# When GpSimd issues the next chunk loads, and where three other transfers stand, in a Perceiver block

## The reference

```python
x = x + softmax(layernorm(x) @ ctx.T) @ ctx              # ctx: 25088 x 2048
h = layernorm(x)
q, k, v = h @ Wq + bq, h @ Wk + bk, h @ Wv + bv          # 32 heads of 64 for q, 8 for k and v
s = softmax(einsum('bsdh,bseh->bsde', q, repeat(k, 4)) / 8)   # 64 x 64 for each token, over the heads
x = x + einsum('bsde,bseh->bsdh', s, repeat(v, 4))
h = layernorm(x)
route = top-2 of softmax(h @ W_gate.T), 8 experts, normalised
x = x + h @ W_base.T + b_base + sum_e route_e * (h @ A_e.T) @ B_e.T   # rank 16
```

## Time and profile before

| | us |
|---|---|
| three runs | 2582.25, 2589.11, 2597.52 (median 2589.11) |
| profiled execution | 2590.12, span 2588.5 |
| busy in the span | PE 2487.6, PEld 2031.1, DVE 1953.2, POOL 1422.9, ACT 1091.7 |
| mean granted clock of TensorE | 0.979 |

### The profile page before, as it was taken

How to read it: one execution, slowest core, us unless ns; L and a number is a source line. 1 busy time by engine, 2 the same in 40 slices (tenths; PEclk the granted TensorE clock), 3 DMA queues, 4 the chain that set the end, 5 groups by cost and what they waited for, 6 DMA issues and landing times.

```text
span 2588.5 us, 36100 instructions
## 1 busy us (share of the span) xinstructions
PE 2487.6 (96%) x11446; PEld 2031.1 (78%) x11446; DVE 1953.2 (75%) x2693; ACT 1091.7 (42%) x1576; POOL 1422.9 (55%) x1060
## 2 busy tenths in 40 slices
PE   6999999999999999999999999999999999997796
PEld 4788888888887888888888888888888888775574
DVE  7888787888877788788888787887878787642335
ACT  4444444444443444444444444444444444333331
POOL 4466666666665556565556655565655555512323
PEclk9999999999999999999999999999999999999877
DMA  9888888787888887898888888888888886685312
GB/s 236 220 219 205 229 205 229 207 228 207 228 216 218 205 216 204 215 220 218 212 223 206 211 209 220 217 205 214 223 216 214 215 220 201 148 155 130 111 61 73
DMA packets 421111, 518.22 MB, mean 200 GB/s; under 512 B 54406, under 2 KB 296070, under 8 KB 418440
## 3 DMA queue, kind: packets, MB, share of 16 engines
q1 hardware_dynamic: 411080, 475.66, 74.7%
q0 software_dynamic: 9984, 41.95, 4.6%
HBM read 488.71 MB, written 28.84 MB: 200 GB/s over the span
## 4 chain that ended last, share of the span: by engine, by line
PE 89%; DMA 4%; DVE 3%; POOL 2%; ACT 1%; issue 1%; SPq 1%; DVEq 0%; ACTq 0%; POOLq 0%
PE ps L1381 29%; PE ps L1383 29%; PE ps L1382 29%; DMA tr<-wt_dram 2%; PE ps L1390 2%; POOL ch_lo L646 1%; DMA raw<-in_ctx_dram 1%; ACT ch_hi L837 1%; DMA tr<-wp_dram 1%; SPq L405 1%; DVE ch_lo L1028 1%; POOL tr L641 0%; POOL x_b L697 0%; DVE tr L1024 0%; DVE acc L1147 0%
## 5 line engine op out<-in xcount | busy, mean ns | idle before, releaser
L578 POOL TENSOR_TENSOR nat_lo<-raw,nat_hi 128x512 fp32r<-128x512 f32 x784 | 1162.5, 1512 | 894.3 <-ACT nat_hi L735 863.3
L1028 DVE TENSOR_TENSOR ch_lo<-tr,ch_hi 128x512 fp32r<-128x512 f32 x784 | 837.8, 1069 | 341.9 <-ACT ch_hi L724 341.8
L724 ACT CAST ch_hi<-tr 128x512 fp32r<-128x512 f32 x784 | 476.3, 621 | 796.7 <-PE ps L1383 788.1
L1381 PE MATMUL ps<-ch_hi,xt_hi 128*128 128x512 f32 x1696 | 681.6, 402 | 24.1 <-DVE ch_lo L1192 9.4
L1382 PE MATMUL ps<-ch_lo,xt_hi 128*128 128x512 f32 x1696 | 665.6, 392 | 0.0
L1383 PE MATMUL ps<-ch_hi,xt_lo 128*128 128x512 f32 x1696 | 665.5, 392 | 0.0
L1381 PE MATMUL ps<-nat_hi,pt_hi 128*128 128x512 f32 x1568 | 614.4, 392 | 8.2 <-DVE pt_lo L977 7.3
L1383 PE MATMUL ps<-nat_hi,pt_lo 128*128 128x512 f32 x1568 | 611.2, 390 | 0.0
L1382 PE MATMUL ps<-nat_lo,pt_hi 128*128 128x512 f32 x1568 | 610.7, 389 | 0.0
L1024 DVE STREAM_TRANSPOSE tr<-quart 128x512 f32<-128x512 f32 x784 | 546.9, 698 | 0.0
L735 ACT CAST nat_hi<-raw 128x2048 fp32r<-128x2048 f32 x196 | 374.5, 1911 | 208.1 <-PE ps L1383 195.1
(11 more groups left out here) (181 smaller groups left out, 1462.5 us busy)
## 6 DMA issues: line engine op xcount, KB each, us to landing
quart<-in_ctx_dram SPq DMA_DIRECT2D x392, 512.0 KB, 8.2
raw<-in_ctx_dram SPq DMA_DIRECT2D x196, 1024.0 KB, 9.0
wq_in<-in_L_attn_Wq_dram POOLq DMA_DIRECT2D x16, 1024.0 KB, 6.4
win<-in_L_ffn_W_base_dram SPq DMA_DIRECT2D x64, 256.0 KB, 6.9
wt_dram<-stage SPq DMA_DIRECT2D x64, 256.0 KB, 7.6
tr<-wt_dram POOLq DMA_DIRECT2D x64, 256.0 KB, 4.2
wq_dram<-wq_out POOLq DMA_DIRECT2D x16, 256.0 KB, 2.3
wp_dram<-stage SPq DMA_DIRECT2D x16, 256.0 KB, 10.1
```

The costliest lines, as they stand in the source:

```text
L578: last = pool.tensor_tensor(nat_lo[:, j, t], raw[:, j % 2, t], nat_hi[:, j, t].bitcast(F32), ALU.subtract)
L724: act.copy(ch_hi[:, c % RING_CH, :], tr[:, c % RING_TR, :]).then_inc(chunk_hi, 1)
L1028: dve.tensor_tensor(ch_lo[:, c % RING_CH, :], tr[:, c % RING_TR, :], ch_hi[:, c % RING_CH, :].bitcast(F32), ALU.subtract).then_inc(chunk_s ...
L1381: pe.matmul(out_, a_hi, b_hi, start=start, stop=False)
```

## The change

POOL's low part of chunk w stands behind the loads of w + 1, w + 2 and w + 3. LoRA's B has its own buffer (8 KB a partition) and is loaded in two halves, at the end of the last two turns; b_base is loaded right behind the q loads. The four turned pieces of W_base use two buffers in turn, and each of the five stores has its own semaphore. The routed sums are transposed after chunks 6 and 7 instead of 11 and 12, v after 9 and 11 instead of 7 and 9. x2 plus b_base is made in eight pieces of 512 columns. The space for the descriptors of GpSimd's transfers is set to 4096 bytes a partition.

```diff
+        stages = (stage, sb("stage_b", [P, 4 * P]))
+        b_nat = sb("b_nat", [P, DC, ER])
...
-        b_nat = put(at_lo + 20 * KIB, "b_nat", [P, DC, ER])
...
-        wt_stored = sem("wt_stored")
+        wt_stored = [sem(f"wt_stored{k}") for k in range(5)]
...
                 if step == 1:
-                    sp.wait_ge(wt_stored, m * 80 + 80)
+                    for k in (3, 4):
+                        sp.wait_ge(wt_stored[k], m * 16 + 16)
                     load_win(m + 1)
...
+            def load_expert(e):
+                sp.dma_start(b_nat[:, :, e * RANK:(e + 1) * RANK],
+                             lora_b[e].rearrange("(o p) r -> p o r", p=P)).then_inc(b_loaded, 16)
+
             next_block(REST[0], LAST_M)
+            for e in range(EXPERTS // 2):
+                load_expert(e)
...
             sp.dma_start(x_nat[:], x_dram).then_inc(x_again, 16)
+            for e in range(EXPERTS // 2, EXPERTS):
+                load_expert(e)
             sp.wait_ge(chunk_transposed, DC * NB)
...
             sp.wait_ge(qkv_done, 3 * TT)
-            for e in range(EXPERTS):
-                sp.dma_start(b_nat[:, :, e * RANK:(e + 1) * RANK],
-                             lora_b[e].rearrange("(o p) r -> p o r", p=P)).then_inc(b_loaded, 16)
-            sp.wait_ge(plain_done, H_B + DC // 4)
             sp.dma_start(b_base_all[:], b_base.unsqueeze(0).broadcast_to([P, OUTF])).then_inc(bias_loaded, 16)
...
-                pool.wait_ge(wt_stored, m * 80 + 64)
+                pool.wait_ge(wt_stored[2], m * 16 + 16)
...
-            lo_base(3)
             pool.wait_ge(qkv_done, 3 * TT)
...
-            for w in range(RING_TR, BASE_W):
-                load_base(w)
-                if by_pool(w):
-                    lo_base(w)
-            for w in range(BASE_W, ALL_W):
-                load_base(w)
-                if by_pool(w):
-                    lo_base(w)
-                if w - BASE_W in X2B_AFTER:
-                    t, half = X2B_AFTER[w - BASE_W]
-                    cols = slice(half * OUTF // 2, (half + 1) * OUTF // 2)
+            for w in range(RING_TR, ALL_W + 3):
+                if w < ALL_W:
+                    load_base(w)
+                if by_pool(w - 3):
+                    lo_base(w - 3)
+                for piece in X2B_AFTER.get(w - 3 - BASE_W, ()):
+                    t, ob = piece // FB, piece % FB
+                    cols = slice(ob * KB, (ob + 1) * KB)
...
                 elif k < 4:
-                    dve.wait_ge(wt_stored, m * 80 + 16 * k)
+                    if k >= 2:
+                        dve.wait_ge(wt_stored[k - 2], m * 16 + 16)
...
-SUM_AFTER = 11
-GSUM_AFTER = 12
-V_AFTER = {7: (0, 1), 9: (2, 3)}
+SUM_AFTER = 6
+GSUM_AFTER = 7
+V_AFTER = {9: (0, 1), 11: (2, 3)}
...
-X2B_AFTER = {7: (0, 0), 9: (0, 1), 13: (1, 0), 15: (1, 1)}
+X2B_AFTER = {7: (0, 1), 9: (2, 3), 11: (4, 5), 13: (6, 7)}
...
-    nc = bacc.Bacc("TRN2", target_bir_lowering=False, num_devices=1)
+    nc = bacc.Bacc("TRN2", target_bir_lowering=False, num_devices=1, dynamic_dma_scratch_size=4096)
```

More of the change, by code:

```diff
@@ L426, in store_turned @@
                 if k < 4:
-                    to, of = wt_dram[4 * k:4 * k + 4, :, bass.ds(m * P, P)], stage
+                    to, of = wt_dram[4 * k:4 * k + 4, :, bass.ds(m * P, P)], stages[k % 2]
                 else:
                     to, of = wp_dram[:, :, bass.ds(m * P, P)], stage2
-                sp.dma_start(to.rearrange("c p o -> p c o"), of[:].rearrange("p (c o) -> p c o", c=4)).then_inc(wt_stored, 16)
+                sp.dma_start(to.rearrange("c p o -> p c o"), of[:].rearrange("p (c o) -> p c o", c=4)).then_inc(wt_stored[k], 16)
             for t in range(TT):
@@ L507, in _ @@
             load_rows(3, ctx_rows(last_row0, 3))
-            sp.wait_ge(wt_stored, 16 * 5 * (LAST_M + 1))
+            for k in range(5):
+                sp.wait_ge(wt_stored[k], 16 * (LAST_M + 1))
             load_w_rows(1, wk_rows)
@@ L681, in _ @@
             pool.wait_ge(v_zeroed, 3)
-            for w in range(RING_TR, BASE_W):
-                load_base(w)
-                if by_pool(w):
-                    lo_base(w)
-            for w in range(BASE_W, ALL_W):
-                load_base(w)
-                if by_pool(w):
-                    lo_base(w)
-                if w - BASE_W in X2B_AFTER:
-                    t, half = X2B_AFTER[w - BASE_W]
-                    cols = slice(half * OUTF // 2, (half + 1) * OUTF // 2)
-                    if half == 0:
+            for w in range(RING_TR, ALL_W + 3):
[6 more added lines that the diff above has]
+                    cols = slice(ob * KB, (ob + 1) * KB)
+                    if ob == 0:
                         pool.wait_ge(x2_ready, t + 1)
-                    if t == 0 and half == 0:
+                    if piece == 0:
                         pool.wait_ge(bias_loaded, 4 * 16)
@@ L1094, in turn_win @@
                 if k < 4:
-                    src, dst = win[:].rearrange("p r (c i) -> p c r i", i=SQ)[:, 4 * k:4 * k + 4], stage
+                    src, dst = win[:].rearrange("p r (c i) -> p c r i", i=SQ)[:, 4 * k:4 * k + 4], stages[k % 2]
                 else:
@@ L1356, in with_base @@
                     piece = slice(ob * KB, (ob + 1) * KB)
-                    if ob % 2 == 0:
-                        dve.wait_ge(x2b_ready, 2 * t + ob // 2 + 1)
+                    dve.wait_ge(x2b_ready, FB * t + ob + 1)
                     link(dve.scalar_tensor_tensor(x2_b[:, t, piece], base_x[:, t, piece], ln3_a[:, t:t + 1], x2_b[:, t, piece],
```

## The result

The changed kernel takes 2527.1 us (median of 4 runs, 2524.1 to 2530.9) against 2592.1 for the kernel before in the same comparison; the ratio is 0.9754 [0.9719, 0.9790]. Run again in a later comparison it took 2534.7 us (5 runs, 2530.4 to 2538.2), ratio 0.9778 [0.9753, 0.9803]. The forecast was 2550 with a range of 2530 to 2574: faster was right, 40 us was too little; it is 58 to 65. The profiled execution took 2524.5 us, its span is 2522.9.

The account below looks back on a forecast made before the run. TensorE was taken to bound the loop, with room only in the tail, where GpSimd's order made chunk loads late. 9 + 17 + 1 + 14 - 1 = 40 us off 2590.1 gave 2550 us, range 2530 to 2574.

Parts of the forecast that it names:

- They remove VectorE's 15 waits: Block loop: two stage buffers and own semaphores remove 23.7 us of VectorE's store waits, worth nothing in time.
- Router: Router's 153 matmuls, 31.0 us at half clock: gain 1 us, bounds 0 and 15.5.
- The clock holds into the router: Rival: with no idle in front, the whole router runs at 2.4 GHz, 14 us more gain, 2536 us; chance 0.10.
- 48 chunks: W_base chunks mixed with attention: unhindered steps give 102.0 against 125.7 us; gain 17 us, bounds 8 and 23.7.
- rival 1: 48 chunks with attention: the attention chain takes the load ring's place as limit; total 2569 us, chance 0.15.
- Summed chunks: Last 16 chunks: TensorE's idle for hw_t and split chunks shrinks; gain 14 us, bounds 10 and 16.
- My walk: Last 16 chunks: event times followed through the new order, with hw at 2549 and hw_t ending at 2554.
- Chunks 0 to 15: First chunks behind the projections: earlier loads and fewer TensorE idles gain 9 us, bounds 4 and 16.
- B goes: First 16 chunks: B's loads leave their place beside chunk 8's late load, which lands about 1.5 us earlier.
- Rival 2: First 16 chunks: chunk loads alternate with SP's transfers, so this stage gains 13 us; total 2546 us, chance 0.20.
- B's loads in the last turns: Loop's end: four B loads delay the last block's third row load; cost 1 us, bounds 0 and 5.
- Descriptor space: GpSimd's queue: cutting descriptor space to 4096 bytes changes nothing, with four loads in flight needing 20 packets per engine.

Follow-up runs that it names:

- experiment 1: Kernel before with only the two stage buffers, their own semaphores and the smaller descriptor space: 2581.7 us against 2590.7, ratio 0.9961.
- experiment 4: Changed kernel with one stage buffer again, the second placed but unused: 2546.1 us, ratio 0.9823.
- experiment 5: Changed kernel with four unused copies on ScalarE ahead of its last bank copy, putting an idle before the router: 2544.1 us, ratio 0.9818.
- experiment 6: Changed kernel with expert picks made by comparing probabilities, without the index search and its cast: 2528.6 us, ratio 0.9756.
- experiment 7: Changed kernel with all eight x2 plus b_base pieces made behind GpSimd's last low part: 2523.2 us, ratio 0.9741.
- experiment 8: Changed kernel with two x2 plus b_base pieces behind chunk 71's low part, six behind the last: 2521.9 us, ratio 0.9740.
- experiment 3: Kernel before with only B's loads moved into the last turns and b_base loaded behind q: 2594.6 us, ratio 1.0005.
- experiment 11: Changed kernel with LoRA's B loaded as before, behind q_t, and b_base behind B's transposes: 2528.5 us, ratio 0.9756.
- experiment 10: Changed kernel once more, unaltered, beside its variants on one chip: 2534.7 us.

## Why the prediction was wrong, step by step

*"They remove VectorE's 15 waits ... from a stretch where TensorE never waits. Nothing either way."* This step failed, and cost 10 of the 25 us. I read 1279.2 busy of 1280 in the earlier trace rows as TensorE at its peak. Its ends are modelled (0.39 us for a matmul whose successor starts 0.23 later), so a wait of 0.2 us leaves no idle in the busy time. The starts and the counts show it. The kernel before, where a block's scores are followed by its weighted sum:

```profile
1014.01 0.39 PE L1382 MATMUL ps<-ch_lo,xt_hi 128*128 128x512 f32 x1
1014.24 0.39 PE L1383 MATMUL ps<-ch_hi,xt_lo 128*128 128x512 f32 x1
1014.68 0.49 PE L1381 MATMUL ps<-nat_hi,pt_hi 128*128 128x512 f32 x1
1015.01 0.40 PE L1382 MATMUL ps<-nat_lo,pt_hi 128*128 128x512 f32 x1
```

0.44 and 0.33 between starts instead of 0.23 and 0.23: 0.3 us lost with no idle. In the same 1280 us the changed kernel does 5755 matmuls, 19 more than the 5736 of the earlier trace rows; 19 x 0.223 = 4.2 us. Most of the rest lay in the first pass over W_base, which my stretch from 870 us left out. The kernel before, its waits from 700 to 870 us, its window from 820 to 840, and TensorE in it:

```profile
DVE stage L1098 <- DMA wt_dram<-stage: 5.4, 1, 5.4
```

```profile
820.00:840.00 20.00, 16.35 (x69) 13.04 (x68) 17.95 (x25) 9.52 (x16) 15.30 (x11) 0.91 0.71 168
```

```profile
834.47 0.49 PE L1381 MATMUL ps<-nat_hi,pt_hi 128*128 128x512 f32 x1 [3.65 <-DVE pt_lo L977]
```

One wait of VectorE of 5.4 us put pt_lo late, TensorE stood 3.65 us and lost clock: 69 matmuls against 94, 25 x 0.223 = 5.6 us. With the 4.2 that is an estimate of 9.8, and experiments 1 and 4 give 10.0 and 11.4 for the loop.

*Router: "The stream did not raise the clock in 31 us, and no row shows whether it would keep it. I take 1."* This step failed too. The stream keeps it. Entered with 0.34 us of idle, the same 153 matmuls took 17.1 us at 1.00 instead of 31.0 at 0.50; experiment 5 puts an idle back and has half clock again. Both levels thus last under this stream for a time, and the idle in front chooses. In the kernel before that idle was more than the 2.98 us: 2.12 us stood 4 us ahead of it, and the granted clock was 0.50 from 2492 to 2493, before the router began. The rival that said so ("The clock holds into the router", 14 more) was right, and its chance of 0.10 too small: two ends of 0 and 15.5 gave no ground to stand at 1. Nor did the prediction say which idle it expected there; its 1.5 us for the bank copy lies between 0.34 and 2.41, where no run shows what this stream does (idles of 1.0 to 1.4 us at the other block ends left the clock at 1.00). This is 13 of the 25 us. The Trainium skill (TensorE: Matmul & The Clock Gate, "Part 1: The HAM clock gate") has the clock at half behind an idle stretch and at full behind a busy one; that it held behind 0.34 us and fell behind 2.41 us agrees in direction.

*48 chunks: 17 of a possible 23.7.* 22.9 came. The ideal of 102.0 from the steps of 6.10 us was the right size, 102.7 came out in every kernel with the new order but two (102.8 and 103.0 count as the same; 104.7 with q late and 104.9 with the added idle). I had kept back nearly 7 us (1.5 at each of four column-block ends, 1 for o_norm) on top of it; the block ends wait 1.0, 1.0, 1.4 and 0.34. The attention chain as the new bound (rival 1) is refuted by the same number.

*Summed chunks: 14; 8.7 came.* My walk put hw at 2549, the loads and casts right, and gave VectorE its old durations. But two operations of 2 and 4 elements a partition took 4.13 and 9.51 us beside GpSimd's low parts and x2 pieces, which the change had put back to back. The failed term is VectorE's chain: hw came 32.4 us into the stage, the walk had 23.8, and with the pieces late it was 23.5. Experiments 6 to 8 show it: the delay stays when the operation is replaced and goes when GpSimd's row is broken up; the stage then takes 24.9 us, a gain of 17.9 on the kernel before.

*Chunks 0 to 15: 9.* The first profile gives 8.2, but by luck. Seven profiles of kernels with this stage's program alike (after, again, experiments 4 to 8) give 44.0, 55.2, 53.9, 48.4, 51.6, 46.3 and 46.9, mean 49.5; three of kernels with the old order (before, experiments 1 and 3) 52.2, 54.8 and 56.5, mean 54.5. The gain is nearer to 5, and the two sets overlap. "B goes" as a part of it was wrong (experiments 3 and 11), q_t as the brake was right. Rival 2, loads alternating with q_t from their issue on, gave this stage 13, which no mean here bears out; how the loads share the queues is not shown.

*B's loads in the last turns: 1.* This step failed, though the table has 1.1 in its place; that is luck. The path was right: the third row load went out 37.2 us behind the last blocks' softmax instead of 29.9, just the 7.3 that the prediction had. But nothing came of it at TensorE. The only idle of over 1 us between that softmax and the last block's end is the same in the kernel before and in experiment 1, neither of which moves B:

```profile
2213.78 0.50 PE L1381 MATMUL ps<-nat_hi,pt_hi 128*128 128x512 f32 x1 [1.56 <-DVE pt_lo L977]
```

```profile
2201.65 0.50 PE L1385 MATMUL ps<-nat_hi,pt_hi 128*128 128x512 f32 x1 [1.56 <-DVE pt_lo L980]
```

These matmuls stand 51.48 and 52.57 us behind the softmax. With one stage buffer and B moved it is 51.48 and 51.51 (experiments 3 and 4); with two buffers it is 52.56 in the changed kernel (at 2202.44) and 52.57 with B not moved (experiment 11). So the 1.1 us goes with the buffers, not with B: it is a part of their 11.5 that does not last, which leaves them 10.4. Four profiles (experiments 4, 5, 10 and 11) lose another 1.6 us behind this point, in the projections, with B moved or not; why is open.

*Descriptor space: nothing.* Right: GpSimd's issues take 0.54 us each and none waits 4 us for a predecessor. That was seen at 4096 bytes only.

Together, by the first profile: 10 (buffers) + 1 (B costs nothing) + 13 (router) + 6 (48 chunks) - 5 (summed chunks) is 25 of the 25.6 us between forecast and measurement; the rest is below 1 us each way. The two steps that carried it out of the range are the buffers' nothing and the router's 1.

What stays open: why the store of q holds SP 16 us in one run and 19 in another, by what rule the chunk loads stand back beside the q loads' pieces, and why a small operation of VectorE is held over GpSimd's whole row in some places and over one operation in others. What a q that never passes through memory would bring was not tried.

## What to carry to other kernels

A busy share of 99.9% is not proof that an engine never waits: compare the starts of successive matmuls, and the number done in equal windows, before a stall elsewhere is priced at nothing, and look at the first pass of a loop too. Where a stretch runs at half clock, ask what the idle in front of it will be after the change; both ends of its price follow from that one gap, and the nearer end is the one whose gap you forecast. When an order is tightened on GpSimd, look for what VectorE does at that moment: leave pauses in GpSimd's row while VectorE has a chain of small operations on the path.

## What the runs showed of the hardware

- VectorE operations of 2 and 4 elements a partition, whose neighbours of that size take 0.15 to 0.17 us, took 4.13 and 9.51 us beside GpSimd operations that stood back to back: a tensor_scalar, a cast and, in the cast's absence, a tensor_tensor. The Trainium skill (SBUF — State Buffer, "Who interferes with whom") says that, for operations which need the pair of ports that VectorE shares with GpSimd, whoever issues first has it "for the whole instruction". The kernel before agrees, with a 128x2 tensor_tensor of 1.16 us that ended 0.02 us behind one GpSimd operation while the next already stood. The cast does not: it was held over seven GpSimd instructions, with one load issue of 0.55 us between them, and ended only behind the last; by the profile's starts it had even begun 0.31 us before the first of them. There the rows decide: a hold can outlast one instruction. Two others, a batch-norm aggregate (0.27 us) and a 128x1 tensor_scalar (0.15 us), ran beside GpSimd's x2 pieces at 2479 us without any delay.
- The 136-column stream of the router kept 2.4 GHz (granted clock 1.00) when it was entered with 0.34 us of idle, and ran wholly at 1.2 GHz (0.50) when entered with 2.98. Entered with 2.41 it fell and came back on the way (0.50 from 2464 to 2480, 1.00 from 2482 to 2484 in experiment 5).
- A 256 KB chunk load lands in 3.1 us by the median; beside the loads of q, ScalarE waited 6 to 17 us for a single one in every profile (6.35 in experiment 11, 16.52 in experiment 1). With LoRA's B behind q, its issues holding SP for 30.04 us, the longest wait was 6.35 and the stage the shortest of all, 42.6 us.
